# A fused transformer layer on one core: the constants' wait of the first patch product, the place and queue of the feed-forward weights, and the order of the first value copies

## The reference, cut to what matters

```python
x = einsum('bnf,df->bnd', patches(data), W_lin) + b_lin
h = concatenate([concatenate([class_token, x]) + position_embeddings, txt])
h = h + attention(layernorm(h))          # rope, |i - j| <= 32, softmax, Wo
h = h + ffn(layernorm(h))                # w1, conv of 3, silu, w2
# weight_quant(w): scale = 1 / clip(mean(abs(w)), 1e-5); clip(round(w * scale), -1, 1) / scale
```

## Time and profile before

| what | value |
|---|---|
| median of 3 runs | 386.39 us (386.0 to 388.16) |
| the profiled execution | 387.26 us, its span 385.4 us |
| TensorE busy | 354.0 us, 92% |
| VectorE, ScalarE, GpSimd busy | 298.3, 271.8, 213.4 us |
| mean granted clock of TensorE | 0.981 |

### The profile page before, as it was taken

The page is one execution under the profiler, slowest core; times in us unless marked ns, Lnnn a source line. Parts: engine busy times, 40 slices in busy tenths (PEclk is TensorE's granted clock), DMA queues, the critical chain, the costliest instruction groups (busy, mean ns, idle before and its releaser), DMA issues.

```text
span 385.4 us, 7870 instructions
## 1 busy us (share of the span) xinstructions
PE 354.0 (92%) x2733; PEld 266.0 (69%) x2733; DVE 298.3 (77%) x639; ACT 271.8 (71%) x555; POOL 213.4 (55%) x245
## 2 busy tenths in 40 slices
PE   7779799999999999999999999999999999977886
PEld 3366557867776797679767867787788677843733
DVE  2156756745699879987998899869977977899795
ACT  3233436668897889778978796889798858872552
POOL 5405599499489947894779349945990025001000
PEclk9899989999999999999999999999999879999999
DMA  7772621101010102011011110111002000100101
GB/s 237 168 168 51 200 82 43 32 15 26 16 25 0 37 20 53 14 25 36 3 33 38 25 48 16 42 32 21 18 20 53 19 2 8 31 0 2 35 0 38
DMA packets 21905, 16.68 MB, mean 43 GB/s; under 512 B 12435, under 2 KB 20936, under 8 KB 21865
## 3 DMA queue, kind: packets, MB, share of 16 engines
q1 hardware_dynamic: 20970, 15.11, 15.7%
q10 hardware_dynamic: 895, 1.06, 1.0%
HBM read 9.82 MB, written 3.38 MB: 34 GB/s over the span
## 4 chain that ended last, share of the span: by engine, by line
PE 50%; ACT 16%; DVE 15%; issue 7%; DMA 6%; POOL 4%; SPq 2%; ACTq 0%; DVEq 0%; POOLq 0%
PE bank L1870 6%; PE bank L1841 5%; PE bank L1884 5%; PE bank L1790 4%; PE bank L1913 4%; PE bank L1943 3%; PE bank L1987 3%; PE bank L1944 3%; ACT shared L1344 3%; PE bank L1861 3%; DMA cst<-in_consts 3%; ACT ctxP L1293 2%; ACT wn L1326 2%; DMA wn<-in_w 2%; PE bank L1737 2%
## 5 line engine op out<-in xcount | busy, mean ns | idle before, releaser
L1507 DVE TENSOR_REDUCE mx<-bank 120x4 fp32r<-120x376 f32 (+3 forms) x88 | 43.0, 505 | 19.4 <-PE bank L1853 18.9
L1273 ACT COPY pT<-bank 94x480 f32<-94x480 f32 (+3 forms) x88 | 47.2, 557 | 9.0 <-PE bank L1870 7.9
L1265 ACT ACTIVATE pr<-bank 120x376 f32<-120x376 f32 (+3 forms) x88 | 38.1, 455 | 21.1 <-PE bank L1861 20.7
L1870 PE MATMUL bank<-cst,pr 120*94 120x120 f32 (+3 forms) x352 | 49.3, 272 | 2.3 <-ACT pr L1265 1.8
L1113 POOL TENSOR_TENSOR rs<-ve,half_neg 110x3 f32<-110x3 f32 x16 | 14.8, 925 | 65.9 <-DVE ve L1535 49.0
L1841 PE MATMUL bank<-kbd,q_hl 128*120 128x376 f32 (+3 forms) x176 | 47.4, 367 | 2.9 <-ACT q_hl L1242 1.9
L1135 POOL TENSOR_TENSOR rc<-qk,cst 110x320 f32<-110x320 f32 x22 | 25.1, 1141 | 35.7 <-ACT qk L1236 35.0
L1943 PE MATMUL bank<-xT_hi,w1T 128*128 128x330 f32 x128 | 42.8, 341 | 1.8 <-DVE late L1590 1.1
L1870 PEld LDWEIGHTS bank<-cst,pr 120*94 120x94 f32 (+3 forms) x352 | 36.5, 122 | 11.3 <-ACT pr L1265 7.0
L1944 PE MATMUL bank<-xT_lo,w1T 128*128 128x330 f32 x128 | 39.4, 314 | 0.0
L1120 POOL TENSOR_SCALAR xn<-h,mv,rs 110x256 f32<-110x256 f32 x21 | 26.6, 1276 | 17.3 <-PE bank L1778 16.9
(11 more groups left out here) (131 smaller groups left out, 872.7 us busy)
## 6 DMA issues: line engine op xcount, KB each, us to landing
kbd<-shared SPq DMA_DIRECT2D x56, 41.2 KB, 2.1
out<-h SPq DMA_DIRECT2D x7, 330.0 KB
wn<-in_w SPq DMA_DIRECT2D x2, 1024.0 KB, 6.8
shared<-in_x SPq DMA_DIRECT2D x4, 432.0 KB
h<-in_txt SPq DMA_DIRECT2D x1, 770.0 KB
late<-in_lin SPq DMA_DIRECT2D x1, 768.0 KB, 7.1
vw<-v_rows SPq DMA_DIRECT2D x8, 94.0 KB
v_rows<-qk SPq DMA_DIRECT2D x8, 82.5 KB
```

The source lines that it names most:

```text
L1265: nc.scalar.activation(pr[:, g % 3, 0:HKV * WIDTH[j]], S_BANKS[g % 2][0:QP, 0:HKV * WIDTH[j]], ACT.Exp, scale=HD ** -0.5).then_inc(exped, 1)
L1273: nc.scalar.copy(pT[0:WIDTH[j], g % 3, :], S_BANKS[g % 2][0:WIDTH[j], 0:HKV * QP]).then_inc(p_kept, 1)
L1507: nc.vector.tensor_reduce(mx[:, g % 4, :].bitcast(F32R), S_BANKS[g % 2][0:QP, 0:HKV * WIDTH[j]].rearrange("p (k c) -> p k c", k=HKV), axis ...
L1870: o = nc.tensor.transpose(S_BANKS[g % 2][0:w, kv * QP:(kv + 1) * QP], pr[:, g % 3, kv * w:(kv + 1) * w], ident[0:QP, 0:QP])
```

## The change

The first patch product waits for the constants and the position rows ahead of its last matmul alone. On ScalarE, the first sort, `keep_pix(0)` and `keep_patch(0)` come ahead of the issues of mask, `wo` and `conv`. The feed-forward weights land in `shared`, over the raw images, and no longer over `pixT`; ScalarE issues them in its own queue at tick 5.5, once three loads are sorted. The absolute sums are four of half a weight each, at the same place in VectorE's order; TensorE adds them up with two matmuls into the last two columns of a bank. SyncE's copy of pair 0's values moves from tick 5 to 1.5, between token parts 1 and 2.

```diff
     'sp.load_v': (
-        (5,),
+        (1.5,),
...
-    'dve.abs_w': (16, 17),
+    'dve.abs_w': (15.1, 15.2, 15.3, 15.4),
...
+    'act.load_w12': (5.5,),
...
-    'sp.load_w12': (4,),
...
-        wabs = sb("wabs", [128, 2])
+        wabs = sb("wabs", [128, 4])
...
+        w1n, at = carve(shared, 0, 128, [MH, D])
+        w2n, at = carve(shared, at, 128, [2, HID])
         u0, at = carve(shared, 0, 128, [MH, T])
...
-        w1n, at = carve(wn, 0, 128, [MH, D])
-        w2n, at = carve(wn, at, 128, [2, HID])
+        at = MH * D + 2 * HID
...
+        sums = Z_BANKS[1][:, 510:512]
...
-            def load_w12():
-                sp.wait_ge(tok_summed, TOKT)
-                sp.dma_start(w1n[:, :, :], w1.rearrange("(m p) d -> p m d", p=128)).then_inc(w12_in, 16)
-                sp.dma_start(w2n[:, :, :], w2.rearrange("(t p) h -> p t h", p=128)).then_inc(w12_in, 16)
...
+            sort_pix_act(0)
+            keep_pix(0)
+            keep_patch(0)
             act.dma_start(mask_sb[:, :], maskbits).then_inc(mask_in, 16)
             act.dma_start(wo_sb[:, :, :], wo_d).then_inc(wts_in, 16)
             act.dma_start(conv[:, :, :], conv_d).then_inc(wts_in, 16)
-            sort_pix_act(0)
-            keep_pix(0)
-            keep_patch(0)
+
+            def load_w12():
+                act.wait_ge(sorted_a, 3)
+                act.wait_ge(sorted_v, 3)
+                act.dma_start(w1n[:, :, :], w1.rearrange("(m p) d -> p m d", p=128)).then_inc(w12_in, 16)
+                act.dma_start(w2n[:, :, :], w2.rearrange("(t p) h -> p t h", p=128)).then_inc(w12_in, 16)
...
-            def abs_w(n):
+            def abs_w(n, half):
                 dve.wait_ge(w12_in, 32)
-                w = (w1n, w2n)[n]
-                nc.vector.tensor_reduce(wabs[:, n:n + 1], w[:, :, :], axis=AX.XY, op=ALU.add,
+                w = w1n[:, half * (MH // 2):(half + 1) * (MH // 2), :] if n == 0 else w2n[:, half:half + 1, :]
+                nc.vector.tensor_reduce(wabs[:, 2 * half + n:2 * half + n + 1], w, axis=AX.XY, op=ALU.add,
                                         apply_absolute_value=True).then_inc(w_absed, 1)
...
                     nc.tensor.matmul(dst, pixT[:, k, lo:hi], wlT[:, k, :], start=(k == 0), stop=False)
+                if s == 0:
+                    pe.wait_ge(consts_in, 16)
+                    pe.wait_ge(pos_in, 16)
                 shift = C_HOT + lo % NPATCH
...
             pe.wait_ge(wlin_in, 16)
-            pe.wait_ge(consts_in, 16)
-            pe.wait_ge(pos_in, 16)
             patch(0)
...
-                pe.wait_ge(w_absed, 2)
-                pe.wait_ge(tok_kept, TOKT - 1)
+                pe.wait_ge(w_absed, 4)
                 pe.wait_ge(v_ones, 1)
-                nc.tensor.matmul(Z_BANKS[1][:, 0:2], ones[:, :], wabs[:, :], start=True, stop=True).then_inc(w_sumall, 1)
+                for half in range(2):
+                    o = nc.tensor.matmul(sums, ones[:, :], wabs[:, 2 * half:2 * half + 2], start=(half == 0), stop=(half == 1))
+                o.then_inc(w_sumall, 1)
```

More of the change, by code:

```diff
@@ L1078, in _ @@
             work = {name: due("sp." + name) for name in (
-                "load_v", "place_k", "move_tok", "load_w12", "store")}
+                "load_v", "place_k", "move_tok", "store")}
             for q in TICKS:
@@ L1086, in _ @@
                     move_tokens(s + 1)
-                for _ in work["load_w12"].get(q, ()):
-                    load_w12()
                 for n, _ in work["store"].get(q, ()):
@@ L1355, in _ @@
             work = {name: due("act." + name) for name in (
-                "exp", "keep_xn", "keep_qk", "keep_q", "keep_ctx", "keep_sel", "quant_x", "high_x", "mid", "keep_p", "keep_k", "tanh", "abs_g", "conv_g", "keep_w", "sort_a", "keep_pix_a", "keep_patch")}
+                "exp", "keep_xn", "keep_qk", "keep_q", "keep_ctx", "keep_sel", "quant_x", "high_x", "mid", "keep_p", "keep_k", "tanh", "abs_g", "conv_g", "keep_w", "sort_a", "load_w12", "keep_pix_a", "keep_patch")}
             for q in TICKS:
@@ L1389, in _ @@
                     sort_pix_act(i + 1)
+                for _ in work["load_w12"].get(q, ()):
+                    load_w12()
                 for i in work["keep_pix_a"].get(q, ()):
@@ L1427, in ternary @@
                     dve.wait_ge(w_sumall, 1)
-                    nc.vector.tensor_scalar(wstat[:, 0:2], Z_BANKS[1][:, 0:2], 1.0 / (HID * D), CLIP_MIN,
+                    nc.vector.tensor_scalar(wstat[:, 0:2], sums, 1.0 / (HID * D), CLIP_MIN,
                                             ALU.mult, ALU.max).then_inc(w_clipped, 1)
@@ L1698, in _ @@
                     keep_pix(i + 1)
-                for n in work["abs_w"].get(q, ()):
-                    abs_w(n)
+                for i in work["abs_w"].get(q, ()):
+                    abs_w(i // 2, i % 2)
                 for s in work["ternary"].get(q, ()):
```

## The result

The changed kernel takes **391.08 us** (median of 4 runs, 389.31 to 392.73); the kernel before, run beside it, takes 386.19 (385.08 to 388.16). The ratio is 1.0121, with a 95% interval from 1.0077 to 1.0164: slower by 4.9 us, forecast 390.6. The profiled execution of after took 392.73 us with a span of 390.8; that of before had 387.26 and 385.4. The four runs of after lie in two pairs, 389.31 and 389.61 at a mean granted clock of 0.98, 392.54 and 392.73 at 0.97 and 0.96, and the profile is the longest of them.

A forecast was written before the change was run, and what follows sets the result against it. TensorE, 92% busy in fixed order, bounds the kernel, so a later start pushes everything. First scores +4.2 us, other terms 0: 387.26 + 4.2 = 391.5, at the median's level 390.6 us; range 389.3 to 392.1.

The forecast's parts named there:

- The sum: Whole kernel: profiled 387.26 us plus 4.2 gives 391.5, or 390.6 us at the level of the median.
- narrow range: Whole kernel's time: the forecast's own range, 389.3 to 392.1 us, given a chance of 0.69.
- The values at tick 1.5: SyncE waits for pair 0's third projection before token part 2, holding ScalarE's copy of part 4: first scores 4.2 us later.
- The first patch: Start on TensorE: first patch's last two matmuls 4.5 us sooner, bounds 0 to 1.64 us gained overall, taken as 0.
- what is late next is SyncE's move of those rows: SyncE at the start: token rows issued 1.64 us sooner, but landing waits for image data, so 0 gained.
- Weights over images: Weights share transfer engines with texts: token part 1 and VectorE's rope 3.6 us late, bounds 0 and 6.2.
- Runs side by side, adds 0: VectorE's 3.6 us rope delay runs beside the 4.2 us from the values; the later one counts, adding 0.
- The absolute sums: VectorE's sums 2.6 us sooner, then TensorE's last pair 1 projection is late: 1.3 gained to 1.1 lost, taken as 0.
- Faster: Rival: SyncE's stop does no harm, part 2 lands before 42.39, gains of 2.9 us remain: 383.5 us, chance 0.05.
- nothing: Rival: the waits at first patch and weights were covered, and so is the new stop: 386.4 us, chance 0.03.
- The start gets through: Rival: token rows land as much sooner as issued, clock stays up behind first scores: 1.3 us later, 387.7, chance 0.11.
- Texts and weights: Rival: weights served ahead of token part 1, VectorE's rope and first scores 6.2 us late: 392.6 us, chance 0.12.

The follow-up runs named there:

- first-patch kernel: Kernel before with only the constants' wait moved to the first patch's last product and ScalarE's three table issues behind its first copies: 386.73 us, ratio 1.0016.
- mended kernels: Two kernels: the mended kernel, 385.15 us, and the same with five more unused matmuls behind the second patch product, 385.10 us.
- filled kernel before: Kernel before with unused matmuls filling TensorE's idle time (17, 5, 5 and 8) and nothing of the change: 389.62 us, ratio 1.0100.
- filled first patch: The first-patch kernel with unused matmuls in TensorE's idle time, 13 behind the first patch product and 11 behind the second turn of pixels: 387.36 us, ratio 1.0014.
- mended kernel: Changed kernel with values at tick 5, weights issued by SyncE behind token part 1, unused matmuls behind first patch, second turn and before first scores: 385.15 us, ratio 0.9960.

## Why the prediction was right

**The sum.** The forecast was +4.2 on the first scores, 390.6 at the level of the median; measured were 391.08 and +4.9, and in the profiled execution +5.27 on the first scores. The time lies inside the narrow range, on the side and by the mechanism that carried most of the chance. That it is within 0.5 us is partly luck: the median lies between two pairs of runs 3 us apart, and the profile shows terms that were off by about 1 us.

**The values at tick 1.5: right, 1.04 short.** Step by step for the first scores (49.62 forecast, 50.66 measured): the third projection was kept at 35.87 and not 35.30 (+0.57); from there to the first window copy it took 2.55 and not 1.98 (+0.57); the six copies and what follows up to part 2 took 4.84 and not 4.94 (-0.10), its fourth issue began 2.34 after the first and not 2.30 (+0.04), it landed in 2.00 and not 2.1 (-0.10); ScalarE began 0.08 after that (+0.08), and 2.98 and not 3.00 passed from its copy to the scores (-0.02). The first of these comes from the start, below. The second fits the weights, which were still landing (share 0.70 from 31 to 38; the second of the two landed 16.7 us after its issue at 21.33, at 38.0): in five kernels whose weights had landed by then, or did so within 0.3 us, that wait was 1.93 to 1.98. The run with the weights issued beside the write-out shows that wait grow to 7.15. That the stop ahead of part 2 is the cause is shown by two runs that put it further back and keep the early weights: against the runs of before made beside them, 3.8 us come back with the values behind part 3, 2.5 with the values behind part 2.

**The first patch: the right number for the wrong reason.** The step that failed is "what is late next is SyncE's move of those rows". I took 0 because the rows would wait for image data. In the first-patch kernel they came 1.26 sooner, most of the 1.64 that was my other bound; in after it was 0.15, and over the ten kernels with this part 0.15 to 1.58. What is late next is TensorE itself. The 4.2 us that it saved ahead of the images turned into idle time, the second patch product then ran at half clock, and pair 0's turn came 0.91 later in after (26.53 against 25.62), 0.77 in the first-patch kernel. I had priced the half clock behind the first scores and not here, though the window at 12 to 18 shows the clock at 0.72 on average, behind an idle stretch of 2.85 us. By the medians the term is still nothing: 1.0016 for this part alone.

**Weights over images: mechanism right, size 1.1 short, and hidden by 2.2 us.** I took 3.6 us for the delay of part 1, the middle of two estimates, between bounds of 0 and 6.2. In after the statistics of pair 1 came 4.70 later than in before. Its part 1 was also issued 0.91 later (27.80 against 26.89), but that did not delay it: in three kernels with the weights elsewhere part 1 was issued at 27.64 to 27.83 and the statistics ran at 32.14 to 32.30. The two others with early weights had their statistics at 35.80 and 37.92: 3.0 and 5.2 later than in before. The Trainium skill's page "DMA: Bandwidth & Descriptors", section "Issuing engines are not separate DMA queues", says that transfers of several issuing engines interleave on the same 16 DMA engines. The trace agrees: the share of the stretch from 21 to 31 rose from 0.81 to 1.06 and token part 1 came late. None of the three shows the whole 6.2 us, which was what I made of the page; it names no size. "Runs side by side, adds 0" held in after; the runs without SyncE's stop show what lay beneath: VectorE's rope then sets the keys, up to 3.2 us later than before.

**The absolute sums: 0, as taken.** The wait for the weights is gone, and the shift comes 9.55 after the first scores where it was 9.67. VectorE is no longer late, TensorE is, as the text named it: its first projection of pair 1 took 2.44 us, hardly less than the 2.55 of before, and the half clock, 10.3 us long around the late scores, covered 5.59 us of its work in place of 3.39. With the clock up and the weights early the distance is 7.70, 1.97 less, where my upper bound was 1.3.

**The rivals.** "Faster" and "nothing" needed part 2 to land before 42.39; it landed at 47.6. "The start gets through" had the rows partly right (0.15 to 1.58 of 1.64) and missed the clock. "Texts and weights" had the right delay and the wrong place: it becomes the bound only when the stop is taken out.

**What stays open.** Where the clock falls in those runs of the mended kernels that end near 385 and later; why token part 1 came 3.0 to 5.2 us late in kernels with the same transfers; why the rows and the weights land later in the filled kernel before. No run answers these.

## What to carry to other kernels

A copy that goes through DRAM and back is a stop in its queue: everything issued behind it inherits the wait for the producer, the write-out and the read-back's issue time, so it goes behind whatever another engine will soon wait for, even if its own reader comes early. Look for a stretch in which the transfer engines idle (here 31 to 38 us, share 0.06) and place a bulk load there, behind the critical small transfer. Here its place in time counted: issued at 21 us by ScalarE the weights made part 1 late (35.80), issued at 34.8 by ScalarE they made part 2 late (ScalarE waited until 43.87), and issued at 31.0 by SyncE, between the two, they held up neither. That a queue of its own is worse than the same place in SyncE's queue was not run. And work taken off the start of TensorE, while it waits for inputs anyway, becomes idle time that can cost the clock of the next step: price the next products at half clock before counting the saving.

## What the runs showed that I had not expected

Pair 0's small write-out took 1.93 us at the least until its reader could go on, and 7.15 where the weights (some 6 us of all engines) were issued half a microsecond ahead of it in the other queue, 7.30 where they were just ahead of it in the same queue. The granted clock fell to 0.50 behind idle stretches that cost nothing by themselves. With one stretch filled, it fell behind the next one, 1.23 us long, in the profiled run of the filled first patch (4.51 us for twelve products that take 2.80) and not behind 1.26 us at the same place in the mended kernel. And unused matmuls alone made the kernel before 1% slower, which the mean clock does not explain: at a mean granted clock of 0.991 two of its runs took 388.75 and 389.07 us, where six runs of the kernel before beside them took 384.77 to 385.88.
